# Local attention's softmax sums moved from the weights to the output of the value matmuls

## The reference, cut to what matters

```
h = shift_token(x)                       # half of the features move one token down
q, k, v = split(h @ wqkv)                # 8 heads of 64
q = rotate(l2norm(q) * qs);  k = rotate(l2norm(k) * ksc)
sim  = einsum('bhwid,bhwjd->bhwij', q * 8, [k of window before, k of window])
attn = softmax(where(mask, -max, sim))   # windows of 64 queries, 128 keys each
o    = einsum('bhwij,bhwjd->bhwid', attn, [v of window before, v of window])
x    = x + o @ wo
...                                      # then a gated feed-forward part
```

## Time and profile before

| what | value |
|---|---|
| median of 3 runs | 1608.4 us (1608.1 to 1611.72) |
| the profiled execution | 1610.09 us |
| its span, first to last instruction | 1608.0 us |
| TensorE busy in the span | 1383.7 us (86%) |
| VectorE busy | 1049.2 us (65%) |
| ScalarE busy | 779.7 us (48%) |
| GpSimd busy | 387.2 us (24%) |
| mean granted TensorE clock | 0.929 of full speed |

### The profile page before, as it was taken

How to read it: one execution, slowest core, us unless ns; L and a number is a source line. 1 busy time by engine, 2 the same in 40 slices (tenths; PEclk the granted TensorE clock), 3 DMA queues, 4 the chain that set the end, 5 groups by cost and what they waited for, 6 DMA issues and landing times.

```text
span 1608.0 us, 25414 instructions
## 1 busy us (share of the span) xinstructions
PE 1383.7 (86%) x9075; PEld 818.4 (51%) x9075; DVE 1049.2 (65%) x2238; ACT 779.7 (48%) x1658; POOL 387.2 (24%) x268
## 2 busy tenths in 40 slices
PE   6999999999999958997799999983688868788866
PEld 4777777777676733332233333322356643466542
DVE  6767767767676663666666676706688744788644
ACT  2444445444454413342245666663477743488731
POOL 2000000000000011345400000001588810688801
PEclk9999999999999978998678999997799979799978
DMA  5000000000000000002023111002000000000000
GB/s 132 1 1 1 0 0 0 0 0 0 0 0 0 0 0 0 1 1 92 12 74 86 40 46 44 5 2 60 1 1 0 1 1 1 1 0 0 1 0 26
DMA packets 23650, 25.44 MB, mean 16 GB/s; under 512 B 5570, under 2 KB 20108, under 8 KB 22284
## 3 DMA queue, kind: packets, MB, share of 16 engines
q1 hardware_dynamic: 23580, 24.51, 5.2%
HBM read 20.11 MB, written 4.39 MB: 15 GB/s over the span
## 4 chain that ended last, share of the span: by engine, by line
PE 62%; POOL 15%; DVE 10%; issue 7%; ACT 4%; DMA 2%; POOLq 0%; SPq 0%; DVEq 0%; ACTq 0%
PE ps L640 14%; PE ps L671 8%; PE ps L682 8%; POOL d_rn L2152 5%; PE ps L952 4%; POOL probsT L2163 4%; PE ps L911 4%; PE ps L932 3%; PE ps L788 2%; POOL q_st L2150 2%; POOL k_st L2150 2%; PE ps L782 2%; PE ps L627 2%; PE ps L772 2%; PE ps L1153 1%
## 5 line engine op out<-in xcount | busy, mean ns | idle before, releaser
L1881 ACT ACTIVATE probsT<-ps 128x512 f32<-128x512 f32 (+1 forms) x304 | 163.7, 576 | 111.0 <-PE ps L936 98.4
L1269 DVE TENSOR_REDUCE negmax<-ps 128x1 f32<-128x1024 f32 x128 | 150.8, 1220 | 76.1 <-PE ps L671 76.1
L1726 ACT ACTIVATE probs<-ps,negmax 128x1024 f32<-128x1024 f32 x128 | 142.8, 1115 | 75.8 <-DVE negmax L1269 75.5
L1732 ACT COPY probsT<-ps 128x512 f32<-128x512 f32 x128 | 75.0, 586 | 177.7 <-PE ps L682 177.7
L682 PEld LDWEIGHTS ps<-ident,probs 128*128 128x128 f32 x1024 | 114.7, 141 | 58.4 <-issue 53.5
L911 PE MATMUL ps<-arena 76*128 76x512 bf16 (+3 forms) x384 | 116.1, 363 | 26.8 <-DVE cmax L1477 20.4
L682 PE MATMUL ps<-ident,probs 128*128 128x128 f32 x1024 | 136.3, 276 | 0.0
L640 PE MATMUL ps<-probsT,v_nat 128*128 128x256 f32 x554 | 129.9, 380 | 0.0
L671 PE MATMUL ps<-k_st,q_st 64*128 64x512 f32 x512 | 127.2, 615 | 2.2 <-DVE v_st L1248 1.4
L1477 DVE CUSTOM_DVE_ANT_0 k_st<-ps,rel 128x256 f32<-128x256 f32 (+7 forms) x128 | 96.8, 756 | 47.9 <-PE ps L911 46.4
L1477 DVE CUSTOM_DVE_ANT_0 q_st<-ps,rel 128x256 f32<-128x256 f32 (+7 forms) x128 | 96.7, 756 | 45.2 <-PE ps L911 44.2
(11 more groups left out here) (259 smaller groups left out, 2665.7 us busy)
## 6 DMA issues: line engine op xcount, KB each, us to landing
arena<-c_parts SPq DMA_DIRECT2D x32, 192.0 KB
arena<-c_parts SPq DMA_DIRECT2D x16, 128.0 KB
arena<-in_L_ffn_w_dram SPq DMA_DIRECT2D x3, 512.0 KB
c_parts<-probsT SPq DMA_DIRECT2D x2, 768.0 KB, 3.5
arena<-in_c_far_dram SPq DMA_DIRECT2D x16, 96.0 KB
c_parts<-work SPq DMA_DIRECT2D x2, 768.0 KB, 11.2
work<-in_L_ffn_wqkv_dram SPq DMA_DIRECT2D x1, 1536.0 KB
x_sb<-in_L_attn_x_dram SPq DMA_DIRECT2D x2, 512.0 KB, 4.8
```

What stands on the lines that cost most here:

```text
L1269: dve.tensor_reduce(negmax[:, u:u + 1], s2, AX_X, ALU.max, negate=True)\
L1726: act.activation(probs[:, u % NPB, :], s2, ACT.Exp, bias=negmax[:, u:u + 1], accum_out=rowsum[:, u:u + 1]).then_inc(s_a_exp, 1)
L1881: act.activation(c_p[:, kt % 2, j0:j0 + heads, q0 - kt * P:q0 - kt * P + n], ps[:, 4 + c % 2, 0:heads * n].rearrange("p (h n) -> p h n", n ...
```

## The change

The softmax weights stay undivided. VectorE takes the reciprocal of the sums of tile t-1 and writes each head's inverse 64 times, as a 128x512 array `d_rr` (queries by inner features); TensorE turns that with four transposes into bank 3, after its value matmuls; ScalarE copies it to `d_R`; and VectorE multiplies the output of the value matmuls (bank 2) by it into `d_o`, where ScalarE copied it before. The reciprocal now stands between the scaled maximum and the copy to `d_pT`, and the sums of squares stand behind the addition into the residual. The copy to `d_vs` goes from VectorE to GpSimd, as a multiplication by ones. GpSimd's multiplication of the weights is gone, and its norm has two waits more. The diff, cut to its core:

```
-        d_rr = sb("d_rr", [P, 2, H2])
+        d_rr = sb("d_rr", [P, INNER])
+        ones_c = sb("ones_c", [P, 1])
+        d_R = pf[:, 7680:8192]
...
 TensorE, step
-                            pe.wait_ge(s_d_z, n - 1)
+                            pe.wait_ge(s_d_Rc, n - 1)
                         pe.matmul(ps[:, 3, :], hv[:, par, :], l_qkv[:, 2 * INNER:3 * INNER],
...
-                        pe.wait_ge(s_d_p, n)
+                        pe.wait_ge(s_d_e, n)
                         for h in range(H2):
                             ins = pe.transpose(ps[:, 4 + h // 4, (h % 4) * P:(h % 4 + 1) * P],
...
-                        pe.wait_ge(s_d_oT, n - 1)
+                        pe.wait_ge(s_d_oT, n)
                         if exists(t, 0):
                             pe.wait_ge(s_d_v, n + 1)
-                        elif t == TILES + 1:
-                            pe.wait_ge(s_d_z, n - 1)
...
                         ins.then_inc(s_d_o, 1)
+                    if exists(t, -1):
+                        pe.wait_ge(s_d_rr, n)
+                        if exists(t, 0):
+                            pe.wait_ge(s_d_v, n + 1)
+                        if exists(t, -2):
+                            pe.wait_ge(s_d_z, n)
+                        for m in range(4):
+                            ins = pe.transpose(ps[:, 3, m * P:(m + 1) * P], d_rr[:, m * P:(m + 1) * P], ident[:, :])
+                        ins.then_inc(s_d_R, 1)
...
 VectorE, step
-                    if exists(t, 0):
-                        if exists(t, -1):
-                            dve.wait_ge(s_d_v, n)
-                            if exists(t, -2):
-                                dve.wait_ge(s_d_o, n - 1)
-                            dve.tensor_scalar(d_vs[WIN:P, par, :], d_va[WIN:P, 1 - par, :], 0.0, None, ALU.add)\
-                               .then_inc(s_d_vs, 1)
...
                     if exists(t, 2):
                         rotate(t + 2, par)
+                    if exists(t, -2):
+                        dve.wait_ge(s_d_o, n - 1)
+                        dve.wait_ge(s_d_Rc, n - 1)
+                        dve.tensor_tensor(d_o[:, par, :, :].rearrange("p m c -> p (m c)"), ps[:, 2, :], d_R,
+                                          ALU.mult).then_inc(s_d_oT, 1)
...
                     if exists(t, -1):
+                        dve.wait_ge(s_d_e, n)
+                        if exists(t, -2):
+                            dve.wait_ge(s_d_R, n - 1)
+                        dve.reciprocal(d_rr[:, :].rearrange("p (m c d) -> p c m d", m=4, c=2),
+                                       d_sum[:, 1 - par, :].rearrange("p (c m) -> p c m", c=2).unsqueeze(3)
+                                       .to_broadcast([P, 2, 4, HD2])).then_inc(s_d_rr, 1)
                         dve.wait_ge(s_d_pt, n)
                         dve.tensor_copy(d_pT[:, 4:8, :].rearrange("p h c -> p (h c)"), ps[:, 5, :])\
                            .then_inc(s_d_pT, 1)
-                    if exists(t, 2):
-                        norms(t + 2, par)
                     if exists(t, -2):
                         dve.wait_ge(s_d_w, n - 1)
                         z = xT[:, bass.ds((t - 2) * P, P)]
                         dve.tensor_tensor(z, ps[:, 3, 0:P], z, ALU.add).then_inc(s_d_z, 1)
+                    if exists(t, 2):
+                        norms(t + 2, par)
...
-                        dve.wait_ge(s_d_e, n + 1)
-                        dve.reciprocal(d_rr[:, par, :], d_sum[:, par, :]).then_inc(s_d_rr, 1)
...
 ScalarE, step
+                    if exists(t, -2):
+                        act.wait_ge(s_d_R, n - 1)
+                        if exists(t, -3):
+                            act.wait_ge(s_d_oT, n - 1)
+                        act.copy(d_R, ps[:, 3, :]).then_inc(s_d_Rc, 1)
                     if exists(t, 0):
                         act.wait_ge(s_d_qkt, n + 1)
...
-                        act.wait_ge(s_d_o, n - 1)
-                        act.copy(d_o[:, par, :, :], ps[:, 2, :].rearrange("p (m c) -> p m c", m=4))\
-                           .then_inc(s_d_oT, 1)
...
 GpSimd, norm of a tile
                     pool.wait_ge(s_d_m, n + 1)
+                    if exists(t, -2):
+                        pool.wait_ge(s_d_qkt, n - 1)
                     pool.tensor_tensor(kq, d_mA[:, par, :], d_mB[:, par, :], ALU.add).then_inc(s_d_add, 1)
                     pool.wait_ge(s_d_cl, n + 1)
+                    if exists(t, -2):
+                        pool.wait_ge(s_d_e, n - 1)
                     pool.tensor_tensor(d_rn[:, par, :], ss[:, par, :], half_c[:, :], ALU.pow).then_inc(s_d_rn, 1)
 GpSimd, step
-                        v = d_p[:, par, :, :]
-                        pool.wait_ge(s_d_rr, T0 + t + 1)
-                        pool.tensor_tensor(v, v, d_rr[:, par, :].unsqueeze(2).to_broadcast([P, H2, P]), ALU.mult)\
-                            .then_inc(s_d_p, 1)
+                        pool.wait_ge(s_d_v, n)
+                        if exists(t, -2):
+                            pool.wait_ge(s_d_o, n - 1)
+                        pool.wait_ge(s_d_kq, n + 2 if exists(t, 1) else n + 1)
+                        v = d_va[WIN:P, 1 - par, :]
+                        pool.tensor_tensor(d_vs[WIN:P, par, :], v, ones_c[WIN:P, 0:1].to_broadcast([P - WIN, INNER]),
+                                           ALU.mult).then_inc(s_d_vs, 1)
...
```

More of the change, by code:

```diff
@@ L423, in build @@
         s_d_rr = sem("s_d_rr")
-        s_d_p = sem("s_d_p")
+        s_d_R = sem("s_d_R")
+        s_d_Rc = sem("s_d_Rc")
         s_d_pt = sem("s_d_pt")
@@ L1510, in _ @@
             ch.link(dve.memset(d_kT[:, :, :, :], 0.0))
+            ch.link(dve.memset(ones_c[:, :], 1.0))
             dve.wait_ge(s_ld_r, 16 * 3)
@@ L1519, in _ @@
             dve.sem_inc(s_d_z, 1)
+            dve.sem_inc(s_d_oT, 1)
             dve.sem_inc(s_d_init, 1)
@@ L1593, in step @@
                     n = T0 + t
-                    if exists(t, 0):
-                        if exists(t, -1):
-                            dve.wait_ge(s_d_v, n)
-                            if exists(t, -2):
-                                dve.wait_ge(s_d_o, n - 1)
-                            dve.tensor_scalar(d_vs[WIN:P, par, :], d_va[WIN:P, 1 - par, :], 0.0, None, ALU.add)\
-                               .then_inc(s_d_vs, 1)
-                        else:
-                            dve.sem_inc(s_d_vs, 1)
                     if exists(t, 2):
                         rotate(t + 2, par)
+                    if exists(t, -2):
[3 more added lines that the diff above has]
+                                          ALU.mult).then_inc(s_d_oT, 1)
                     if exists(t, 0):
@@ L2159, in step @@
                 def step(t, par):
-                    if exists(t, 0):
-                        v = d_p[:, par, :, :]
-                        pool.wait_ge(s_d_rr, T0 + t + 1)
-                        pool.tensor_tensor(v, v, d_rr[:, par, :].unsqueeze(2).to_broadcast([P, H2, P]), ALU.mult)\
-                            .then_inc(s_d_p, 1)
+                    n = T0 + t
+                    if exists(t, -1):
+                        pool.wait_ge(s_d_v, n)
[5 more added lines that the diff above has]
+                                           ALU.mult).then_inc(s_d_vs, 1)
+                    else:
+                        pool.sem_inc(s_d_vs, 1)
                     if exists(t, 2):
+                        pool.wait_ge(s_d_vs, n + 1)
                         unit_norm(t + 2, par)
```

## The result

The changed kernel takes **1727.42 us** (median of 4 runs, 1722.42 to 1728.72) against 1608.25 us (4 runs, 1606.33 to 1611.72): ratio 1.0733, 95% interval [1.0705, 1.0761]. The forecast was 1669 us, range 1648 to 1700. Slower was right; the loss is +119 us where +60.5 us was forecast.

A forecast was written before the change was run, and what follows sets the result against it. No engine was full; a chain of waits through GpSimd's multiply and VectorE's copy bounded the kernel. Steps 49.5, layer ends 6.0 and clock 5 gave +60.5 us: 1669 us against 1608.4, range 1648 to 1700.

The forecast's parts named there:

- the loop: Chain from one maximum to the next through VectorE's reciprocal, TensorE and ScalarE: 11.22 us a step, +49.5 us in all.
- the ends: Last maximum to last residual add of each layer: 17.0 us instead of 13.97, +3.0 us a layer, 6.0 summed.
- the price of the division: VectorE's reciprocal of 512 columns, at 6.25 ns a column, takes 3.35 us instead of 0.20.
- Rival 4: VectorE's reciprocal costs more at 512 columns, 6.9 ns a column or 3.7 us: total 1680 us; chance 0.04.
- rival 2: VectorE's reciprocal costs like any 512-wide operation: steps 9.5 us, 1604 us, or 1587 if ScalarE's inverse copy hides; chance 0.07.
- no cost: GpSimd's two new waits queue its norm work later, free because the result is used two steps on.
- rival 3: GpSimd's add (2.51 us) holds VectorE's reciprocal: up to 2.4 us more in each of 28 steps, 1736 us; chance 0.06.
- the clock: TensorE idles 3.5 us in steps 13 to 15, then runs at half speed: 5 us for six gaps, 0 to 10.
- Rival 5: TensorE's clock falls in every step, not the last three: up to 1.7 us x 28, 1717 us; chance 0.03.
- The held copy in the 10.00 us step: Before the change, VectorE's 64-row copy takes 2.11 us instead of 0.42 beside GpSimd's multiply, making the long step.

## Why the prediction was right or wrong

**Right: the loop.** The clean step of the timeline above, from the maximum at 1288.85, against the pieces that were summed:

| piece | forecast | measured, from starts |
|---|---|---|
| maximum to weight copy, with the reciprocal | 1.34 + 3.27 = 4.61 | 1293.55 - 1288.85 = 4.70 |
| weight copy to value matmuls | 0.79 | 1294.27 - 1293.55 = 0.72 |
| value matmuls | 1.17 | 1295.37 - 1294.27 = 1.10 |
| transposes of the inverses | 0.45 | 1295.86 - 1295.37 = 0.49 |
| next tile's transposes to its maximum | 1.10 + 1.28 + 1.82 = 4.20 | 1299.91 - 1295.86 = 4.05 |
| sum | 11.22 | 11.06 |

With hold and clock both taken away (1664.92) the loss is 56.0 us against the 1608.96 us of the kernel before on the same chip. The forecast had 49.5 for the steps and 6.0 for the ends, 55.5; the end alone, forecast at 17.0 us, is 16.84. That the totals agree within 0.5 us is partly luck: by stretches of the profiled runs the steps cost 23.1 and 23.8 us more and the ends some 3 us each, 53 in all; the rest lies outside the two loops.

**Right: the price of the division.** 3342 ns against 3.35 us. Rival 4's steeper slope and rival 2's cheap reciprocal fall on the group's row.

**Wrong: no term for a held instruction other than the reciprocal.** This is the step that failed, worth 43 to 52 us; with the hold taken away the kernel takes 1675.24 us, 6 more than forecast. In the prediction's own terms, GpSimd's new order was put at "no cost", because its result is used two steps on, and what its add would come to stand beside was asked in rival 3 alone. Rival 3 had the mechanism, the place (the add beginning about when the reciprocal does) and the right size of a full hold (2.4 us forecast, 2.36 measured). But it named the reciprocal as the one held, and asked only whether that one could be. Its 1736 us lies near the measured 1727 partly by luck: the mean hold was 0.8 us (984 less 167 ns), and the lower clock brought the rest. Directly ahead of the reciprocal stood the scaling, and the kernel before already showed short instructions held for a long one: the copy (0.42 and 2.11 us), and the clamp of the sums of squares, 16 columns wide, which took 0.17 us at 1221.18 and 0.78 at 1231.17, beside GpSimd's scaling of k. Its group there:

```profile
L1590 DVE TENSOR_SCALAR ss<-ss 128x16 f32<-128x16 f32 x32 | 17.7, 553 | 1.1
```

The sentence of the Trainium skill that rival 3 gave (GPSIMD Engine Reference, section "Specifications") names two inputs from SBUF; the scaling has them, the reciprocal has one.

**Mis-sized: the clock, forecast 5 us (0 to 10).** It is 10.3 us with the hold away, from the steps up to tile 15 and the layer ends, where the idle time in one piece is 3.46 us (3.5 forecast): the upper end of its range. With the hold it is 19.3, because held steps idle TensorE for longer ahead of the value matmuls. In the changed kernel's two loops the four such gaps of 1.75 to 1.86 us were followed by no fall of the clock; of the 26 from 2.19 us up, 23 met or were followed by stretches of 3.4 or 6.8 us at the lower level. In the kernel with the extra matmuls 7 of 16 gaps of 2.06 to 2.49 us did, so the length of a gap alone doesn't decide. Rival 5 said that the clock would fall in every step, and it did in most, but as a consequence of the hold: its case against, that the clean step's idle time does nothing, holds in the clean steps.

**Not borne out, without effect on the sum: what set the steps before.** The held copy in the 10.00 us step was read as part of the loop. Taking it away, by a wait that also delays the multiply, changed nothing. The sum did not rest on it, as it counted from the measured 132 us. What remains is the chain through GpSimd's multiply, add, power and scale that spans two steps; that is argued from the rows and was not tried by itself.

**Right: rival 2's other figures.** With a cheap way to spread the inverses, and the add out of the way, steps are 9.53 us (forecast 9.5, ScalarE's copy in it) and the total is 1607.4 (forecast 1604). The end gains 1.86 us (13.97 to 12.11; forecast 2.1). Hiding that copy, which rival 2 priced at 17 us, gave 7.4 (1607.40 to 1600.00), as TensorE's 9.3 us come next.

## What to carry to other kernels

A reciprocal on VectorE is paid by the columns it writes: invert the few numbers first and spread them with a copy, 0.20 + 0.43 us here instead of 3.34. When an instruction of GpSimd moves in time, list every VectorE instruction that it can come to stand beside, the shortest ones too, and give each the length of GpSimd's instruction if its kind can be held; a wait for the right semaphore, or another kind of instruction in that place, takes the cost away. Ask of a stall that was seen in the trace whether anything ended later because of it, before its removal is counted as a gain.

## What the runs showed that had not been expected

- An instruction of 8 columns and 167 ns was held for up to 2.36 us, all of GpSimd's 2.35 us add, and the hold, with the lower clock it brought, cost 52 us of 1727.
- The hold works both ways: a VectorE copy that began with the add went first, and the add took 2.65 us instead of 2.35.
- Hold and clock feed one another: taking both away gave 62.5 us (1727.42 to 1664.92), of which 52.2 came with the hold's removal and only 10.3 after it, while the clock's remedy alone gave 19.3 and made the hold's mean rise from 984 to 1449 ns.
